# Macaron block (FFN, butterfly mixer, FFN) on 8 cores: how the blocks of T are prepared beside the units, where the second chunk joins, and what the second FFN's first slabs wait for

## The chip, the cores and the metric

One Trainium2 chip, all 8 cores. Each core runs the same program on its own 2048 of the 16384 tokens, with no exchange between cores. The metric is the device time of the slowest core in microseconds (us), lower is better.

## The reference, cut to what matters

`x` is 16384 tokens (4 x 4096) of 2048 channels, float32. `fwht` is the normalised Walsh-Hadamard transform over the last axis.

```python
def ffn(x):                       # _L0_ffn_ref
    x = fwht(x * SU_ug) / SCALE                       # this is T, 2048 wide
    x_up   = x @ W_up.T   * (Wscale_ug[:INTER] * SCALE)    # 8192 wide
    x_gate = x @ W_gate.T * (Wscale_ug[INTER:] * SCALE)
    x = silu(x_gate) * x_up
    x = fwht(x * SU_dp) / SCALE
    return x @ W_down.T * (Wscale_dp * SCALE)

def mixer(u):                     # _L0_attn_ref
    state = apply_butterfly(u @ W_b_rank @ W_b_state, A_factors)   # rank 64, 256 states
    return state @ W_c_rank @ W_c_model + D_vec * u

x = x + 0.5 * ffn(layernorm(x))
x = x + mixer(layernorm(x))
x = x + 0.5 * ffn(layernorm(x))
```

The same FFN weights serve both FFNs.

## The kernel before, in words

**Layout.** Channels lie on partitions, tokens on the free axis. A core's 2048 tokens are 8 blocks of 256 (`PB`), 4 sets `s` of 512 (`SC`), and 2 chunks `c` of 1024. `place(j)` is the j-th 8 KB (per partition) of the big buffer BIG; T of chunk 0 lies in places 0 to 6, T of chunk 1 in places 7 to 13. Behind them come three slabs of weights (`SL`, `NSLAB`), the slabs' sums (`SUMS`) and scratch.

**A program with a plan.** All instructions are put out by one Python program that appends to five lists, one for each engine (`Prog.st`, `Prog.dma`). A wait is on the count that another instruction leaves in a semaphore. The order of each engine's list is fixed there. Work in the background is a set of generators (`put`); `tick(us)` moves a planned clock on and resumes each generator whose time has come, and `yield 3.0` in one of them means: go on not before 3 us later. A bare `yield` means the next tick. The main stream calls `tick(8 * MM)` = 1.73 us after each 8 matmuls, so times are rounded up to ticks of 1.73. The planned clock sets only the order of the lists; on the chip each engine runs its list as its semaphores allow.

**Preparing T.** Each block goes through `norm` (two casts on ScalarE, 16 matmuls with ones, two subtractions on VectorE, two squares, 16 matmuls, square root, reciprocal) and `transform` (8 groups of two matmuls with the Hadamard matrix and an eviction, then butterflies for distances 8, 4, 2 and 1, an add and a subtract each over 2048 columns, L376 and L379), and is stored to `tsc` with a DMA of the SP queue. `prep_first` does it for the first FFN: it asks for x (`x_halves`, two DMAs on SP), yields 45 us times `S.pace`, then norm and transform. `prep_mixed` does norm, the mixer, the store of x2, norm and transform. A set of buffers (`Set`) serves one block at a time: S0 (PXF, PXC, PXA) takes the even blocks, S1 (inside the places of chunk 1) the odd ones in the first FFN, S2 in the second, until set 3, whose two blocks (6 and 7) both go through S0 beside the second FFN's units. `S.pace` is 0.4 for blocks 2 and 3 and goes back to 1.0 in `t7_rest` when they are done.

**Up product (`u_phase`).** 64 tiles of 128 + 128 rows of W_up and W_gate. A slab (`load`, L84 through POOL's queue, 2 MB of float32 cast to 1 MB of bf16) holds one tile. A unit is one tile with one chunk as a Strassen product (`strassen`, L694): 7 products of 8 matmuls of 128x512, with 6 combination adds on VectorE (L703), one copy and two silu on ScalarE and two multiplications (L862) on VectorE. It needs 5 sums of the slab (`sums`, L779, VectorE), made once per slab, and 5 sums of T over two halves each (`t7_sums`, L662). In the first FFN tiles 0 to 11 (`ALONE`) run first with set 0 alone as plain products (L797). Then tiles up to `FIRST[f]` run with chunk 0 alone, then chunk 1 **joins**: from tile `FIRST[f]` on each slab serves both chunks; after tile 63 the early tiles are loaded again for chunk 1 alone, and the early 12 for set 1 and chunk 1. So `FIRST` = 32 gives 64 + 20 + 24 = 108 slabs, 36 in the second FFN 64 + 36 = 100.

**The join.** When chunk 1 is first needed, `need` waits in the plan until its four blocks are stored, puts `t7_build` (four loads of T, a pause of 20 us, ten sums) and ticks until it is done. `need1` is the same for the second FFN.

**Beside it.** `side0` runs blocks 2, 4 and 6 in S0, waits for T of chunk 1, and then runs `fold`: W_down is transformed in 64 units of 8 matmuls (L507), casts (L511), a load and a store each (`wdn` to `fsc`, then `fsc` to `dsc`). The down product of the first FFN (`d_phase`, L971) reads `dsc` through a ring of four places (`ring_emit`, SP queue) and holds the preparation of sets 0 to 2 of the second FFN. At its end `ahead` puts `head()`, the `start` of the second FFN's `u_phase`, which loads slabs 0, 1 and 2 at planned distances of 14 us. The second FFN's down product is `Down7` (L1194).

## Time and profile before

| what | us |
|---|---|
| three runs | 5574.59, 5505.05, 5411.33 (median 5505.05) |
| the profiled execution, its own time | 5411.29 |
| its span on the slowest core (5) | 5409.7 |
| spans of the other cores | 5380.2 to 5404.4 |

| stage on core 5 | from | to |
|---|---|---|
| blocks 0 and 1, then tiles 0 to 11 with set 0 | 0 | 171 |
| chunk 0 alone, blocks 4 to 7 beside it | 171 | 524 |
| both chunks, fold beside them | 524 | 1425 |
| chunk 1 alone, the fold's end beside it | 1425 | 1580 |
| rest of the up product | 1580 | 1920 |
| down product, preparation of the second FFN | 1920 | 2926 |
| second FFN: chunk 0 alone, blocks 6 and 7 | 2926 | 3433 |
| both chunks | 3450 | 4108 |
| chunk 1 alone | 4108 | 4545 |
| second down product | 4545 | 5410 |

How to read the rows. PE is TensorE (matmuls), PEld its weight loads, DVE VectorE, ACT ScalarE, POOL GpSimd, SP the sync engine; a name with q is that engine's queue of DMA issues. L694 is a line of the kernel; most DMAs are issued by one helper at L84. `out<-in` are buffers. "PEclk" is the granted TensorE clock as a share of full speed, "DMA" the mean busy share of the core's 16 DMA engines. In a timeline a row is start, length, engine, line, operation, and in brackets the idle time before it and what ended it. In the waits a row says who waited for whom: total us, times, longest. Ends of matmuls are modelled and overlap, so times per matmul are taken from counts over a stretch or from starts. A few records of matmuls may be missing.

### The profile page before, as it was taken

What the parts mean: (1) busy time and instruction counts of PE and PEld (TensorE: products, weight loads), DVE (VectorE), ACT (ScalarE), POOL (GpSimd) and SP (SyncE); (2) the same over time, 40 slices, a digit from 0 to 9 for tenths busy, and PEclk for the clock granted to TensorE, in tenths of its full rate; (3) what the DMA queues carried; (4) which work ended last, traced back from release to release, by engine and by line L of the source; (5) the groups of instructions that cost most, each with busy time, mean ns of one, the idle gap of its engine ahead of it and who ended that gap; (6) DMA issues with size and microseconds to landing.
All of it is one profiled execution on the core that took longest, in us unless ns stands there. A gap on an engine that the chain in (4) does not pass through costs nothing.

```text
span 5409.7 us, 69392 instructions; the slowest of 8 cores (5380.2 to 5409.7 us)
## 1 busy us (share of the span) xinstructions
PE 5124.2 (95%) x23972; PEld 2350.6 (43%) x23972; DVE 3118.1 (58%) x4405; ACT 1011.2 (19%) x1460; POOL 128.6 (2%) x247
## 2 busy tenths in 40 slices
PE   6788999999999999999998999999999999997998
PEld 3343444444444444444453444444444444443443
DVE  5777455555563611243345787655557776766766
ACT  3221343444331100111110222111111111000000
POOL 0000000000000000000000000000000000000000
PEclk8999999999999999999999999999999999998999
DMA  7566888877987766686856556332335555776765
GB/s 164 102 131 134 169 190 177 193 199 187 210 185 143 160 206 216 225 277 212 289 193 163 105 119 152 76 68 61 69 63 129 109 111 157 233 221 213 244 221 187
DMA packets 378590, 901.16 MB, mean 167 GB/s; under 512 B 30150, under 2 KB 259526, under 8 KB 311494
## 3 DMA queue, kind: packets, MB, share of 16 engines
q1 hardware_dynamic: 224760, 512.43, 30.2%
q0 software_dynamic: 34992, 252.00, 27.5%
q10 hardware_dynamic: 118496, 132.29, 7.0%
q8 instruction: 200, 3.28, 0.3%
q14 instruction: 142, 1.16, 0.1%
HBM read 918.95 MB, written 229.64 MB: 212 GB/s over the span
## 4 chain that ended last, share of the span: by engine, by line
PE 76%; DMA 10%; DVE 8%; issue 4%; ACT 1%; SPq 1%; ACTq 0%; DVEq 0%; POOLq 0%; POOL 0%
PE P L694 44%; PE P L971 15%; PE P L1194 11%; PE P L797 2%; DMA BIG<-dsc 2%; PE P L281 2%; DMA PXF<-fsc 2%; PE P L507 2%; DVE BIG L703 1%; DMA fsc<-PXC 1%; SPq L84 1%; DMA fsc<-PXA 1%; DVE BIG L779 1%; DVE BIG L1209 1%; DMA PXF<-wdn 1%
## 5 line engine op out<-in xcount | busy, mean ns | idle before, releaser
L694 PE MATMUL P<-BIG 128*128 128x512 bf16 x13664 | 3074.2, 381 | 78.6 <-DVE BIG L703 50.9
L694 PEld LDWEIGHTS P<-BIG 128*128 128x128 bf16 x13664 | 1338.0, 98 | 1703.6 <-issue 138.0
L971 PE MATMUL P<-BIG 128*128 128x512 bf16 x4096 | 903.6, 380 | 33.0 <-DMA BIG<-dsc 33.0
L703 DVE TENSOR_TENSOR BIG<-P,BIG 128x512 f32<-128x512 f32 x976 | 670.2, 687 | 287.1 <-PE P L694 124.0
L703 DVE TENSOR_TENSOR BIG<-BIG,P 128x512 f32<-128x512 f32 x488 | 333.7, 685 | 537.9 <-ACT BIG L872 452.0
L779 DVE TENSOR_TENSOR BIG<-BIG 128x1024 bf16<-128x1024 bf16 x920 | 615.1, 684 | 36.5 <-DMA BIG<-wug 18.2
L971 PEld LDWEIGHTS P<-BIG 128*128 128x128 bf16 x4096 | 399.8, 98 | 511.9 <-issue 51.2
L1194 PE MATMUL P<-BIG 128*128 128x512 bf16 x1792 | 399.3, 384 | 28.6 <-DVE BIG L1209 22.0
L872 ACT ACTIVATE BIG<-P,WSCG 128x512 bf16<-128x512 f32 x244 | 168.1, 689 | 902.0 <-PE P L694 901.9
L862 DVE SCALAR_TENSOR_TENSOR GST<-P,WSCU,BIG 128x512 bf16<-128x512 f32 x244 | 183.1, 750 | 250.2 <-ACT BIG L877 238.9
L1194 PEld LDWEIGHTS P<-BIG 128*128 128x128 bf16 x1792 | 175.9, 99 | 249.1 <-issue 45.7
L707 ACT COPY BIG<-P 128x512 f32<-128x512 f32 x244 | 144.2, 591 | 718.0 <-DVE BIG L779 331.0
L1194 PE MATMUL P<-BIG,PXF 128*128 128x512 bf16 x1024 | 236.2, 385 | 25.5 <-DVE BIG L1209 23.6
L937 DVE SCALAR_TENSOR_TENSOR BIG<-P,WSC,BIG 128x512 f32<-128x512 f32 x64 | 45.1, 746 | 365.0 <-PE P L971 365.0
L877 ACT ACTIVATE BIG<-BIG,WSCG 128x512 bf16<-128x512 f32 x244 | 176.1, 722 | 275.8 <-DVE BIG L703 275.8
L862 DVE SCALAR_TENSOR_TENSOR GST<-BIG,WSCU 128x512 bf16<-128x512 f32 x244 | 183.4, 752 | 42.9 <-DVE BIG L703 42.9
L84 POOL DMA_DIRECT2D BIG<-wug x208 | 109.8, 528 | 4063.6 <-PE P L694 2041.3
L511 ACT CAST PXC<-P 128x512 bf16<-128x512 f32 x256 | 146.3, 586 | 276.8 <-PE P L507 184.4
L511 ACT CAST PXA<-P 128x512 bf16<-128x512 f32 x256 | 146.5, 586 | 275.3 <-PE P L507 188.1
L1209 DVE TENSOR_TENSOR BIG<-P,BIG 128x512 f32<-128x512 f32 x184 | 125.7, 686 | 124.3 <-PE P L1194 121.6
L797 PE MATMUL P<-BIG 128*128 128x512 bf16 x768 | 169.3, 381 | 21.3 <-DVE BIG L368 20.2
L1223 ACT COPY BIG<-P 128x512 f32<-128x512 f32 x46 | 26.9, 586 | 829.6 <-PE P L1194 570.6
(101 smaller groups left out, 2385.2 us busy)
## 6 DMA issues: line engine op xcount, KB each, us to landing
BIG<-wug POOLq DMA_DIRECT2D x208, 1024.0 KB, 10.0
BIG<-dsc SPq DMA_DIRECT2D x133, 1024.0 KB, 7.0
gsc<-GST ACTq DMA_DIRECT2D x512, 128.0 KB, 7.3
PXF<-wdn POOLq DMA_DIRECT2D x32, 1024.0 KB, 11.7
PXF<-fsc SPq DMA_DIRECT2D x32, 1024.0 KB, 9.1
BIG<-gsc SPq DMA_DIRECT2D x32, 1024.0 KB, 6.7
BIG<-gsc SPq DMA_DIRECT2D x128, 256.0 KB, 6.8
outT<-BIG ACTq DMA_DIRECT2D x92, 256.0 KB, 4.7
```

The lines of the kernel that those rows point to most:

```text
L84: (lambda e, o=out, i=in_: e.dma_start(out=o, in_=i), ws, (sem, 16)))
L511: t_ev = p.st("scalar", lambda e, b=b, i=i, j=j: e.copy(fou[j][:, i * 512:(i + 1) * 512], PS[b][:, :]), [t, out_tok[j]])
L694: tok[j] = p.st("tensor", lambda e, k=k, l=a(j, k), r=b(j, k): e.matmul(PS[bank][:, :], l, r, start=(k == 0 and not acc), stop=(k == n - 1 ...
L703: return p.st("vector", lambda e: e.tensor_tensor(o, x, y, op), waits)
L779: tk[j] = p.st("vector", lambda e, o=o, x=x, y=y, op=op: e.tensor_tensor(o, x, y, op), [sl_tok[i], sum_free[i % 2], tk.get(2) if j == 6 el ...
L797: "tensor", lambda e, b=b, c0=c0, k=k: e.matmul(PS[b][:, :], L[:, c0:c0 + 128], t7_cols(T[k // 8], k % 8), start=(k == 0), stop=(k == NKT ...
L862: tg = p.st("vector", lambda e, t=t: e.scalar_tensor_tensor(g, src, WSCU[:, t:t + 1], sl, OP.mult, OP.mult), x + [t_vec, gst_tok[slot]])
L872: cb["s1"] = p.st("scalar", lambda e, t=t: e.activation(si[0], PS[where][:, :], AF.Silu, scale=WSCG[:, t:t + 1]), [tok, tmp["s1"], t_wscg])
L877: ts = p.st("scalar", lambda e, t=t: e.activation(si[1], where, AF.Silu, scale=WSCG[:, t:t + 1]), [tok, tmp["s2"], t_wscg])
L971: t9=t9: e.matmul(PS[b][:, :], W[:, c0:c0 + 128], gr, start=t0, stop=t9),
L1194: tok[j] = p.st("tensor", lambda e, l=l, r=r, m=m: e.matmul(PS[bank][:, :], l, r, start=(m == a and not acc), stop=(m == b - 1), skip_grou ...
L1209: return p.st("vector", lambda e: e.tensor_tensor(o, x, y, op), waits)
```

## The change

- A block's set asks for x of its next block (`next(first[blk + 2])`, in the second FFN `next(after)`) right behind its norm; the yield of 45 us (30 us) that follows the request is used up there.
- `Set` gets a `step`: each step of `transform` yields `S.step` us, in place of the next tick. `paced` runs blocks 2 and 3 as before, then blocks 4 to 7 with pace 1.2 and step 4.0. Set 3 of the second FFN runs with pace 1.3 and step 4.0.
- `t7_build` of chunk 1 is no longer put at the join: it follows the last block in `side0` (ahead of `fold`) and in `last()`. Its four loads go out 6 us apart and its ten sums 3 us apart.
- `FIRST` goes from (32, 36) to (36, 48): 112 slabs in each FFN.
- In the second FFN slabs 1 and 2 wait for the load of the ring that was issued last.

```diff
--- before.py
+++ after.py
@@ -21,7 +21,7 @@
 NRING = 4
 NITEM = 10
 NSLAB = 3
-FIRST = (32, 36)
+FIRST = (36, 48)
 ALONE = (12, 0)
 MM = 0.216
 C8192 = 1.0 / float(np.sqrt(8192.0))
@@ -290,7 +290,7 @@
                 self.X, self.XC, self.A, self.RS, self.i = x, xc, xa, rs, i
                 self.b0, self.b1 = banks
                 self.x_free, self.xc_free, self.a_free, self.rs_free = [], [], [], []
-                self.pace = 1.0
+                self.pace, self.step = 1.0, 0.0
 
         def kh(ap):
             return ap.rearrange("p (k t) -> p k t", k=8)
@@ -352,7 +352,7 @@
                     bc(S.RS, 2), OP.mult), [t, t_v, t_rs])
                 ps_free[b] = [t_ev]
                 t_pe = t
-                yield
+                yield S.step
             S.rs_free = [t_ev]
             src, dst = A, XC
             tl = [t_ev, t_pe]
@@ -375,12 +375,12 @@
                 dv = dst.rearrange("p (n h w) -> p n h w", h=2, w=dc * PB)
                 t1 = p.st("vector", lambda e, sv=sv, dv=dv: e.tensor_tensor(
                     dv[:, :, 0, :], sv[:, :, 0, :], sv[:, :, 1, :], OP.add), tl)
-                yield
+                yield S.step
                 t2 = p.st("vector", lambda e, sv=sv, dv=dv: e.tensor_tensor(
                     dv[:, :, 1, :], sv[:, :, 0, :], sv[:, :, 1, :], OP.subtract))
                 tl = [t2]
                 src, dst = dst, src
-                yield
+                yield S.step
             S.xc_free = [t2]
             t = p.dma("sync", sPT[S.i], tsc[f][blk], A, [t2])
             S.a_free = [t]
@@ -398,9 +398,11 @@
             yield 45.0 * S.pace
             t_xc, t_v, t_rs = yield from norm(S, t_x, False)
             S.x_free = [t_xc]
+            if 4 <= blk + 2 < NBLK:
+                next(first[blk + 2])
             yield from transform(S, 0, blk, t_xc, t_v, t_rs)
 
-        def prep_mixed(S, blk):
+        def prep_mixed(S, blk, after=None):
             s = blk // 2
             X, XC, A = S.X, S.XC, S.A
             t_x = x_halves(S, x1s, blk, [S.x_free, x1_tok[s]])
@@ -452,6 +454,8 @@
             yield 3.0
             t_xc, t_v, t_rs = yield from norm(S, [t_x2, t_x2], False)
             S.x_free = [t_xc, t_st]
+            if after is not None:
+                next(after)
             yield from transform(S, 1, blk, t_xc, t_v, t_rs)
 
         spad_free = [None, None]
@@ -671,8 +675,9 @@
             tk = {}
             for j in (1, 4, 5, 6):
                 tk[j] = t7_load(f, c, j, [free.get(j)])
-            yield 20.0
-            yield from t7_sums(c, tk, free, (0, 2, 3, 5, 6))
+                yield 6.0
+            for _ in t7_sums(c, tk, free, (0, 2, 3, 5, 6)):
+                yield 3.0
             toks[c] = tk
 
         def t7_cols(slot, k):
@@ -823,7 +828,8 @@
 
             def start(waits=()):
                 for i in range(3):
-                    load(i, waits)
+
+                    load(i, waits if al or i == 0 else ring_tok[-1:])
                     yield 0.0 if al else 14.0
                 yield from sums(0)
 
@@ -1281,7 +1287,6 @@
         def t7_rest():
             while len(t_tok[0][1]) < 2:
                 yield
-            S0.pace = S1.pace = 1.0
             tk = {j: list(t_tok[0][j in (4, 5)]) for j in (1, 4, 5, 6)}
             st5 = p.dma("sync", sPT[0],
                         tsc[0][2:4, :, 0:2048].rearrange("b p x -> p b x"),
@@ -1293,10 +1298,7 @@
                 yield
             yield from t7_sums(0, tk, {6: alone_over[0]}, (6,))
 
-        def need(f, c, free):
-            wait_t(f, c)
-            if c == 1:
-                put(t7_build(f, c, toks, free()))
+        def need(c):
             while toks[c] is None:
                 tick(2.0)
 
@@ -1321,7 +1323,7 @@
                 if pos < 8:
                     gpos[0][pos] = g_load(0, 0, pos, pos)
 
-        up = u_phase(0, toks, lambda c: need(0, c, set1_over), ring_a, ring_b)
+        up = u_phase(0, toks, need, ring_a, ring_b)
         head = next(up)
         put(first[0])
         put(first[1])
@@ -1331,14 +1333,22 @@
         t_wbrb = p.dma("gpsimd", sC[1], WBRB[:, :], wbr)
 
 
+        def paced(S, gens):
+
+            yield from gens[0]
+            S.pace, S.step = 1.2, 4.0
+            yield from in_turn(gens[1:])
+            S.pace, S.step = 1.0, 0.0
+
         def side0():
-            yield from in_turn([first[2], first[4], first[6]])
-            while toks[1] is None:
+            yield from paced(S0, [first[2], first[4], first[6]])
+            while len(t_tok[0][2]) < 2 or len(t_tok[0][3]) < 2:
                 yield
+            yield from t7_build(0, 1, toks, set1_over())
             yield from fold()
 
         put(side0())
-        put(in_turn([first[3], first[5], first[7]]))
+        put(paced(S1, [first[3], first[5], first[7]]))
         put(t7_rest())
         for _ in up:
             pass
@@ -1356,7 +1366,13 @@
                 put(late(prep_mixed(S0, 2 * s)))
                 put(late(prep_mixed(S2, 2 * s + 1)))
             else:
-                put(late(in_turn([prep_mixed(S0, 2 * s), prep_mixed(S0, 2 * s + 1)])))
+                def last():
+                    yield 10.0
+                    S0.pace, S0.step = 1.3, 4.0
+                    final = prep_mixed(S0, 2 * s + 1)
+                    yield from in_turn([prep_mixed(S0, 2 * s, final), final])
+                    yield from t7_build(1, 1, toks1, item2[0])
+                put(last())
 
         def before(s):
             if s == 0:
@@ -1370,8 +1386,6 @@
         item2 = []
 
         def need1(c):
-            wait_t(1, c)
-            put(t7_build(1, c, toks1, item2[0]))
             while toks1[c] is None:
                 tick(2.0)
```

## Rows read from the trace of the kernel before

**Rows 1.** The page: PE's busy time, and its granted clock in 40 slices

```profile
PE 5124.2 (95%) x23972; PEld 2350.6 (43%) x23972; DVE 3118.1 (58%) x4405; ACT 1011.2 (19%) x1460; POOL 128.6 (2%) x247
...
PEclk8999999999999999999999999999999999998999
```

**Rows 2.** Windows by stage: from:to, length, busy us (x instructions), PEclk, DMA share, GB/s

```profile
171.00:524.00 353.00, 292.78 (x1371) 134.90 (x1368) 263.95 (x357) 78.27 (x88) 11.61 (x22) 0.94 0.61 122
...
1425.00:1580.00 155.00, 149.44 (x683) 67.05 (x682) 93.38 (x143) 60.22 (x107) 5.80 (x11) 0.99 0.98 223
...
2926.00:3433.00 507.00, 480.99 (x2296) 223.84 (x2296) 400.57 (x584) 116.90 (x142) 19.01 (x36) 0.99 0.58 124
3433.00:3450.00 17.00, 15.75 (x60) 6.41 (x61) 16.10 (x19) 1.66 (x3) 0.00 (x0) 0.81 0.01 4
3450.00:4108.00 658.00, 658.00 (x3050) 298.31 (x3049) 385.08 (x575) 108.60 (x164) 14.77 (x28) 1.00 0.34 73
```

**Rows 3.** Windows of line L694 alone, PE

```profile
171.00:524.00 353.00, 270.24 (x1176) 0.94 0.61 122
2926.00:3433.00 507.00, 461.18 (x2072) 0.99 0.58 124
```

**Rows 4.** Timeline of PE near 213 us: start, length, engine, line

```profile
212.25 1.91 PE L281 MATMUL P<-PXA,ONES 128*128 128x256 bf16 x16
213.99 1.91 PE L281 MATMUL P<-BIG,ONES 128*128 128x256 bf16 x16
```

**Rows 5.** Waits of PE, 171 to 545 us: total, times, longest

```profile
PE P L694 <- DVE BIG L703: 34.5, 14, 5.8
PE P L281 <- ACT PXA L308: 13.3, 1, 13.3
PE P L694 <- DVE BIG L662: 5.5, 1, 5.5
```

**Rows 6.** Timeline of PE, waits in brackets: up to the first join

```profile
184.76 3.57 PE L281 MATMUL P<-PXA,ONES 128*128 128x256 bf16 x16 [13.31 <-ACT PXA L308]
...
404.31 7.41 PE L694 MATMUL P<-BIG 128*128 128x512 bf16 x24 [5.44 <-DVE BIG L703]
...
524.54 10.62 PE L694 MATMUL P<-BIG 128*128 128x512 bf16 x40 [5.52 <-DVE BIG L662]
```

**Rows 7.** Windows of 20 us, one of a burst on VectorE

```profile
400.00:420.00 20.00, 12.36 (x40) 4.73 (x41) 18.73 (x23) 1.41 (x2) 0.53 (x1) 0.74 0.36 65
```

**Rows 8.** Timeline of SP: when x is asked for

```profile
109.31 0.85 SPq L84 DMA_DIRECT2D PXF<-ub  x2
...
273.24 3.40 SPq L84 DMA_DIRECT2D PXF<-ub  x2
```

**Rows 9.** Timeline of DVE at the first join

```profile
522.04 11.82 DVE L662 TENSOR_TENSOR BIG<-BIG 128x2048 bf16<-128x2048 bf16 x10
```

**Rows 10.** Windows of 100 us, one of single units with nothing beside them

```profile
4300.00:4400.00 100.00, 100.00 (x465) 45.34 (x464) 70.60 (x108) 16.68 (x25) 4.76 (x9) 1.00 0.56 107
```

**Rows 11.** Tile wug, 180 to 430 us

```profile
DMA to landing us min/median/max: 8.3/9.9/22.0
```

**Rows 12.** Timeline of PE: two waits of the fold's matmuls

```profile
588.82 0.59 PE L507 MATMUL P<-PXF,H128B 128*128 128x512 bf16 x1 [8.45 <-ACT PXC L511]
...
1431.60 0.38 PE L507 MATMUL P<-PXF,HKB 128*128 128x512 bf16 x1 [2.98 <-DMA PXF<-fsc]
```

**Rows 13.** Timeline at the end of the first down product, and its DMA issues

```profile
2871.02 1.59 POOL L84 DMA_DIRECT2D BIG<-wug  x3 [999.66 <-DVE BIG L379]
...
2889.40 7.07 PE L971 MATMUL P<-BIG 128*128 128x512 bf16 x32 [1.59 <-DMA BIG<-dsc]
2907.43 15.47 PE L971 MATMUL P<-BIG 128*128 128x512 bf16 x64 [10.96 <-DMA BIG<-dsc]
...
BIG<-dsc SPq DMA_DIRECT2D x4, 1024.0 KB, 23.5
BIG<-wug POOLq DMA_DIRECT2D x3, 1024.0 KB, 24.3
```

## The prediction, made before the change was run

> **What bounds the kernel now.** I read the page first, then the windows by stage, then the waits and the timeline of the stages that fall short. The page gives PE 95% busy, and a clock granted in full except in a few slices [rows 1]; the reader is to see that nothing is to be gained where PE runs through. The windows by stage give the measure of running through: 3050 matmuls of 128x512 in 658 us, 0.2157 us each, at clock 1.00 and no idle time [rows 2]. A Strassen unit has 56 of them, so 12.08 us. A matmul of 128x256 takes 1.74 us for 16, 0.109 us each (the distance of the two starts) [rows 4]. With these two prices each stage has a floor.
>
> The stage ahead of the first join (171 to 524 us) holds 1371 matmul records, 1176 of them L694, which is 21 units [rows 2, 3]; the other 195 are norms and transforms of x. Floor: 1176 x 0.2157 + 195 x 0.109 = 253.7 + 21.3 = 275. It takes 353, so 78 us are lost. The same stage of the second FFN (2926 to 3433) holds 2072 of L694, 37 units, and 224 others [rows 2, 3]: 446.9 + 24.4 = 471.3 of 507, 35.7 lost. The 17 us behind it hold 60 matmuls, 12.9 us worth: 4.1 lost [rows 2]. These two stages are all that the larger parts of the change touch.
>
> What is lost in the first: PE waits 34.5 us in 14 pieces for VectorE's combination adds, 13.3 us once for a cast on ScalarE, and 5.5 us for the sums of T at the join [rows 5]. The timeline shows where: at 184.8 (the cast), at 404 amid a burst, at 524.5 (the join) [rows 6]. In the burst VectorE is 18.73 of 20 us busy, and the granted clock is 0.74 [rows 7]: the engine idled just before, so the loss has a second part, matmuls at the lower of the two levels. Bursts come from the generator of `transform`: it gives one butterfly half at every tick of the plan (1.73 us), for both sets at once.
>
> **Part by part.** *Prefetch of x and pacing (first FFN).* The row of SP shows that x of blocks 4 and 5 was asked for at 109.3, as soon as the norm before had freed X, though its instruction stands behind the whole transform; x of blocks 6 and 7 was asked for at 273.2, behind the store of T [rows 8]. So for blocks 4 and 5 nothing moves in time on SP; for 6 and 7 the two loads of each set leave ahead of the store that they stood behind. What changes is the plan: each of blocks 4 to 7 loses its 45 us of planned waiting, and its steps are spread: norm 9 yields of 3.6 to 4.8 us (5.18 us each when rounded up to ticks), transform 16 of 4.0 (also 5.18), so 130 us a block instead of some 106. Blocks 2 and 3 end at planned 59 us, blocks 4 to 7 then take 260 (to 319), the T build 4 x 6.9 + 10 x 3.46 = 62 (to 381). The join is planned at 12 x 6.91 + 25 x 12.1 = 385. So T of chunk 1 is there in time, with nothing to spare.
>
> VectorE pays for it: it was busy 264 us in the stage [rows 2]. To that come 11.8 us for the ten sums of T, now inside the stage [rows 9], and four more units with their slab sums at 8.5 us each (70.6 us for 465/56 = 8.3 units [rows 10]), 34 us: 310. PE's floor with 25 units is 275 + 48.3 = 323. VectorE at 0.96 of PE's floor is the tight point of the change. Where it is fullest now it reaches 0.94 [rows 7], and 310/0.94 = 330, so at least 7 us are lost. From above: if its share of the stage stayed at 264/353 = 0.748, the stage would take 310/0.748 = 414, with 91 lost. The nearest row is the second FFN's stage, with one stream of preparation beside single units and a share of 0.79: it loses 7.3% of its floor on top, 35.7 of 471 [rows 2]; 7.3% of 323 is 24. I add 9 for what stays of the cast's wait at 185 (its x is ready sooner, but VectorE still waits for a store of T there) and take 33, between 12 and 91. Before, the same 25 units ended at 353 + 3.5 (the matmuls after the wait at the join, 40 in 10.62 us [rows 6], and a small wait) + 48.3 = 404.8 from the stage's start; now 323 + 33 = 356. **Gain 48.5 us**, 70 at best, a loss of 9 at worst.
>
> What is late next at the join: the plan is tight, so one or two sums of T may be put out with no unit between them, 2 us; it is in the 9. The four loads of T now go out 6 us apart, in place of four at once, so the slab that they share the DMA engines with is less delayed.
>
> The Trainium skill speaks against this part: "SBUF — State Buffer" (the box on the trap where DVE blocks DMA) says that a DMA issued from GpSimd's queue waits for its descriptors while VectorE runs an instruction in a two-port mode. The slabs are issued there, and VectorE gets fuller. The trace does not bear it out as a cost: in this stage, with VectorE at 0.75 and up to 0.94, a slab landed in 9.9 us at the median and 22.0 at most [rows 11]. By the rule a slab would be late; with three in flight it has some 36 us, so the sum is the same by the one and by the other unless landings double.
>
> *FIRST (first FFN), 32 to 36.* Four more slabs (208 to 212), their loads and 20 sums, hidden where nothing else runs: the row of single units has PE 100 of 100 us busy with VectorE at 0.71 [rows 10]. But the fold keeps its length (512 ticks, some 73 units) while the joint stage has 8 units fewer, so 8 more units of chunk 1 alone run beside the fold. That pairing has a row: 1425 to 1580, DMA share 0.98, 683 matmuls, floor 147.3 of 155, so 7.7 us lost over 11.4 units [rows 2], 0.68 a unit. **Cost 5.5 us.** From below it is nothing; from above it is a wait like that of the fold's matmul at 588.8, 8.45 us, behind a store of the fold, where later ones waited 2.98 [rows 12].
>
> *Second FFN: step, x of the last block, T build, 36 to 48.* One stream. Planned: 10 + 245 + 210 for two blocks, 62 for T, 527 in all, against a join at 49 x 12.1 = 593: 66 us to spare, so the join's wait goes for certain (5.5 us of wait and its slow matmuls are within the 35.7 + 4.1). VectorE: 400.6 + 12 x 8.5 + 11.8 = 514 of a floor of 471.3 + 145 = 616, 0.83. Bounds: at best 8 us lost, at worst its share stays at 0.79 and 651 are needed, 35 lost. The bursts are gone and the density hardly rises: I take 20 lost. Before 40 were: **gain 20 us**, from 5 to 32. The 12 more slabs and their 41 us of sums lie in stages where PE never waited.
>
> *Slabs 1 and 2 behind the ring.* At 2871.0 all three slabs are issued while the down product still needs two loads of its ring; these take 23.5 us at the median, and PE waits 1.59 and 10.96 us for them, the last until 2907.4 [rows 13]. With two of three megabytes of weights moved behind the last ring load, that one should land about ten microseconds sooner. Both waits go, and some 2 us of matmuls at the lower clock. POOL's queue now waits for the last ring load with slabs 1 and 2; behind them stands only slab 3, which needs slab 0's unit to end. Slab 1 is needed one unit after slab 0, 12 us later, and is asked for before the stage begins. **Gain 14 us**, from 0 (if the loads of T beside it are what delays the ring) to 15.
>
> **Sum.** 48.5 - 5.5 + 20 + 14 = 77 us. The profiled execution took 5411.3 us (span 5409.7), so 5334 us. The three runs shown lie from 5411 to 5575 with a median of 5505, 94 us above the profiled one; the forecast is for an execution like the profiled one, and at the place of that median the same gain reads 5428.
>
> **Rivals.** *A, VectorE does not get fuller.* Its steps stand in one program with PE's, and each sum put between two combination adds delays the release of a bank; then the share of each stage stays. First stage 414 against 404.8 (loss 9), second 651 against 656 (gain 5), ring 14, fold -5.5: gain 4, 5407 us. For it: PE's 34.5 us of waits are all of this kind, and two sets still step at the same tick. Against: they come in bursts, with stretches of 20 us at full rate between.
>
> *B, the smooth plan works as in the best stretches.* First stage loses 12 (gain 70), second 8 (gain 32), ring 14, fold -3: 113 us, 5298. For it: with full use the clock stays up; against: VectorE at 0.96 of PE's floor.
>
> *C, slower: the fold beside single slabs.* DMA share is 0.98 there already. If the backlog grows over 19 units instead of 11, each of the some 6 or 7 fold units in the 8 added ones waits like the one at 588.8, 8.45 us and the clock's fall behind it (0.26 of 20 us, 5.2): 7 x 13.7 = 96 against a gain of 82: 5425 us. It decides from 12 us a fold unit. Against: waits there were 3 us and less.
>
> *D, the prefetch does nothing:* on SP it does nothing for blocks 4 and 5, as said; this is in the forecast.
>
> **Chances.** The forecast 0.57 (its own range 5300 to 5370), A 0.20, B 0.17, C 0.06. The range goes from 5280 (within B) to 5435, which takes in A, C and the place of the median. Faster by over 2% (about what a measurement of this kernel can tell from no change) means under 5303: all of B and a small part of the forecast, 0.22. Slower by over 2% would need C with twice its price: 0.04. Within 2%: 0.74.
>
> **What would show it.** Right: no wait of PE for L662 at either join; 25 units in some 356 us from 171 us on with VectorE near 0.87; no wait of L971 for dsc near 2890 to 2907; the windows beside the fold's end at 0.98 DMA share and over 430 matmuls in 100 us. Wrong: new waits of PE for L703 spread evenly over the first stage (A), waits for fsc in every fold unit behind the joint stage (C), or a wait for slab 1 or 2 at the start of the second FFN.

## The result, and the profile after

| | before | after |
|---|---|---|
| median | 5505.05 us | 5467.2 us (5 runs) |
| lowest | 5411.33 us | 5383.99 us |
| ratio, 95% interval | 1 | 0.9935 [0.9910, 0.9960] |
| profiled execution, own time | 5411.29 us | 5383.99 us |
| its spans, mean of 8 cores | 5393.95 us | 5363.2 us |

So the change is a gain of some 35 us by the ratio (0.0065 x 5411), and 27 us between the two profiled executions, where 77 was forecast. Some executions, both medians among them, are disturbed (the cores of a die at a lower granted clock) and are left out of comparisons; the only profiles of the experiments `e1_ring` (on cores 0 to 3) and `e7_step0` fell in such executions and are read only as far as said there.

The page of after, PE's busy time and clock, beside [rows 1]; the page numbers lines some 5 higher now (L699 is the Strassen matmul, L708 its combination add, L784 a slab's sum, L712 its copy, L868 the multiplication, L977 the down product, L802 and L818 the plain product of tiles 0 to 11 and its multiplication, L511 and L515 the fold's matmul and cast; L666 is the sum of T).

```profile
PE 5122.2 (95%) x23972; PEld 2350.1 (44%) x23972; DVE 3163.0 (59%) x4485; ACT 1011.7 (19%) x1460; POOL 137.6 (3%) x263
...
PEclk8999999999999999999999999999999999998999
```

PE's work is the same 23972 matmuls. VectorE has the 80 instructions of 16 more slabs. The stage ahead of the first join, now with 36 - 12 = 24 units and the first of the join, and the window beside the fold, answering to [rows 2]; below them L699 alone in the first, as [rows 3].

```profile
171.00:562.00 391.00, 342.22 (x1610) 156.20 (x1609) 305.95 (x418) 79.51 (x96) 14.84 (x28) 0.97 0.60 126
...
1300.00:1400.00 100.00, 98.05 (x452) 43.98 (x451) 57.43 (x87) 40.76 (x73) 3.18 (x6) 1.00 0.95 219
1400.00:1500.00 100.00, 95.69 (x442) 42.87 (x441) 59.65 (x91) 39.21 (x70) 3.71 (x7) 1.00 0.98 224
```

```profile
171.00:562.00 391.00, 319.73 (x1414) 136.99 (x1415) 0.97 0.60 126
```

VectorE's busy time, 306 us, is what was forecast (310). The length isn't: 391 us for 1414 / 56 = 25.25 units, with VectorE at 306 / 391 = 0.78. Of the 196 other matmuls 36 are 128x512 ones of L802 and L511 and 160 are 128x256, so the floor is 1450 x 0.2157 + 160 x 0.109 = 330, and 61 us are lost. What PE waited for in it, as [rows 5], and where, as [rows 6]:

```profile
PE P L699 <- DVE BIG L708: 28.4, 23, 4.9
PE P L699 <- DVE BIG L784: 14.0, 1, 14.0
PE P L699 <- ACT BIG L712: 6.2, 7, 1.5
```

```profile
177.62 0.81 PE L802 MATMUL P<-BIG 128*128 128x512 bf16 x3
192.46 3.15 PE L699 MATMUL P<-BIG 128*128 128x512 bf16 x7 [14.03 <-DVE BIG L784]
```

The wait for the cast at 184.8 is gone, and at the same place stands one of 14.0 us for a slab's sum. The waits for combination adds are shorter and more: 28.4 us in 23 pieces after 34.5 in 14. No wait for a sum of T at the join is left. VectorE's timeline shows what the slab's sum stood behind:

```profile
172.91 2.56 DVE L666 TENSOR_TENSOR BIG<-BIG 128x2048 bf16<-128x2048 bf16 x2 [7.14 <-DMA tsc<-BIG]
175.38 2.28 DVE L317 TENSOR_TENSOR PXC<-PXF,P 128x2048 bf16<-128x2048 f32 x1
177.58 2.28 DVE L317 TENSOR_TENSOR BIG<-BIG,P 128x2048 bf16<-128x2048 f32 x1
179.78 0.75 DVE L818 SCALAR_TENSOR_TENSOR GST<-P,WSCU,BIG 128x512 bf16<-128x512 f32 x1
185.44 0.75 DVE L818 SCALAR_TENSOR_TENSOR GST<-P,WSCU,BIG 128x512 bf16<-128x512 f32 x1 [4.91 <-ACT BIG L812]
186.10 2.28 DVE L317 TENSOR_TENSOR PXC<-PXF,P 128x2048 bf16<-128x2048 f32 x1
188.30 2.28 DVE L317 TENSOR_TENSOR BIG<-BIG,P 128x2048 bf16<-128x2048 f32 x1
190.49 1.22 DVE L666 TENSOR_TENSOR BIG<-BIG 128x2048 bf16<-128x2048 bf16 x1
191.63 0.69 DVE L784 TENSOR_TENSOR BIG<-BIG 128x1024 bf16<-128x1024 bf16 x1
```

Four L317 (the norm's subtractions of blocks 4 and 5, 2.28 us each) now stand in VectorE's list ahead of the first sums of the first Strassen slab, and the whole list waited 7.14 us behind a sum of T for a store.

Where T of chunk 1 is built, first SP, then VectorE:

```profile
475.44 2.88 SPq L84 DMA_DIRECT2D BIG<-tsc  x4
...
DMA to landing us min/median/max: 17.0/34.6/42.9
```

```profile
506.20 1.22 DVE L666 TENSOR_TENSOR BIG<-BIG 128x2048 bf16<-128x2048 bf16 x1 [6.52 <-DMA BIG<-tsc]
...
516.38 1.23 DVE L666 TENSOR_TENSOR BIG<-BIG 128x2048 bf16<-128x2048 bf16 x1 [2.90 <-DMA BIG<-tsc]
```

The four loads go out together (they all wait for the last store of T, whatever the plan puts between them), land 17.0 to 42.9 us later, and the sums, planned 3 us apart, wait for them at the head of VectorE's list: combination adds stand behind.

The end of the down product, as [rows 13], with its issues of loads:

```profile
2859.53 0.53 POOL L84 DMA_DIRECT2D BIG<-wug  x1 [1009.43 <-DVE BIG L379]
2892.58 1.06 POOL L84 DMA_DIRECT2D BIG<-wug  x2 [32.52 <-DMA BIG<-dsc]
```

```profile
2889.45 15.91 PE L977 MATMUL P<-BIG 128*128 128x512 bf16 x64 [6.22 <-DMA BIG<-dsc]
2908.83 8.79 PE L699 MATMUL P<-BIG 128*128 128x512 bf16 x40 [3.46 <-DVE BIG L784]
```

```profile
BIG<-dsc SPq DMA_DIRECT2D x4, 1024.0 KB, 18.5
```

POOL holds slabs 1 and 2 back 32.5 us as meant; the ring's load lands sooner (18.5 after 23.5 us at the median), but not in time: PE still waits 6.2 us for it.

**A clock by stages.** To compare eleven kernels I take, on each core, the issue of the slab that a unit's end releases (POOL's timeline), and the mean over the 8 cores. A: tiles 0 to 11 done. J: the first tile done with both chunks, which is tile 36 where the join is at 36; where it is at 32 (39), four (three) units of 12.08 us are added (taken off), so that the work up to J is the same 26 units. U: the last slab of the first up product. R: the first unit of the second FFN. K: as J for the second join, at 48. E: the last slab of the second FFN.

| kernel | A | J | U | R | K | E |
|---|---|---|---|---|---|---|
| before | 170.5 | 586.6 | 1856.7 | 2928.5 | 3582.1 | 4493.7 |
| after | 177.9 | 568.4 | 1847.4 | 2912.1 | 3551.9 | 4463.3 |
| e2_ffn1 | 177.6 | 572.9 | 1854.8 | 2926.0 | 3579.4 | 4490.9 |
| e3_ffn2 | 170.6 | 587.9 | 1862.1 | 2936.8 | 3575.2 | 4487.2 |
| e4_norm_late | 170.1 | 574.1 | 1855.7 | 2917.1 | 3555.4 | 4466.9 |
| e6_t_later | 177.5 | 565.9 | 1845.3 | 2911.3 | 3553.6 | 4465.1 |
| e8_first32 | 177.8 | 580.2 | 1871.3 | 2939.5 | 3577.9 | 4489.6 |
| e9_step0_held | 177.8 | 588.5 | 1876.8 | 2939.5 | 3577.5 | 4488.9 |
| e10_no_butterfly | 177.0 | 542.7 | 1828.5 | 2895.0 | 3539.6 | 4451.0 |
| e11_hold | 177.3 | 551.3 | 1833.5 | 2898.4 | 3536.2 | 4447.6 |
| e12_hold_gap | 177.5 | 548.5 | 1834.2 | 2901.0 | 3546.0 | 4457.3 |

Each row is one execution, and two pairs show how far such rows can be trusted. `e2_ffn1` has after's instructions up to U, and its J is 4.5 us later (3.3 of them from the first Strassen unit) and its U 7.4 us later; `e3_ffn2` has before's, and its J is 1.3 and its U 5.4 us later. Differences below some 5 us at J and 7 us at U therefore show nothing by themselves.

The difference of after and before, stage by stage, against the terms of the forecast's sum:

| stretch | gain, us | forecast |
|---|---|---|
| start to J | 18.2 | 48.5 |
| J to U | -8.9 | -5.5 |
| U to R | 7.1 | 14 |
| R to K | 13.8 | 20 |
| K to E | 0.2 | 0 |
| sum | 30.4 | 77 |

The sum agrees with the 30.8 us by which the mean span fell. Every term has its sign and gives less than forecast; two thirds of what is missing is in the first. The 3.4 us between -8.9 and -5.5 are within the scatter just given.

### The profile page after: what moved, and what is told of

Read it like the earlier page. It is cut to its first block, busy times and chain, and to the rows that moved or that the text cites. A ratio compares the mean times of both kernels' runs of the same rounds, so it can differ in the third digit from the quotient of the medians.

```text
span 5382.3 us, 69545 instructions; the slowest of 8 cores (5332.6 to 5382.3 us)
## 1 busy us (share of the span) xinstructions
PE 5122.2 (95%) x23972; PEld 2350.1 (44%) x23972; DVE 3163.0 (59%) x4485; ACT 1011.7 (19%) x1460; POOL 137.6 (3%) x263
## 3 DMA queue, kind: packets, MB, share of 16 engines
q1 hardware_dynamic: 224760, 512.43, 30.4%
## 4 chain that ended last, share of the span: by engine, by line
PE 78%; DMA 8%; DVE 7%; issue 4%; ACT 1%; SPq 1%; ACTq 1%; DVEq 0%
PE P L699 45%; PE P L977 15%; PE P L1200 11%; PE P L802 2%; DMA BIG<-dsc 2%; PE P L281 2%; PE P L511 2%; DVE BIG L708 1%; DMA fsc<-PXA 1%; DMA PXF<-fsc 1%; SPq L84 1%; DMA BIG<-tsc 1%; DVE BIG L784 1%; DVE BIG L1215 1%; DMA tsc<-BIG 1%
## 5 line engine op out<-in xcount | busy, mean ns | idle before, releaser
L699 PE MATMUL P<-BIG 128*128 128x512 bf16 x13664 | 3065.2, 380 | 72.5 <-DVE BIG L708 43.1
L699 PEld LDWEIGHTS P<-BIG 128*128 128x128 bf16 x13664 | 1334.8, 98 | 1690.0 <-issue 122.0
L977 PE MATMUL P<-BIG 128*128 128x512 bf16 x4096 | 906.5, 381 | 33.8 <-DMA BIG<-dsc 33.8
L708 DVE TENSOR_TENSOR BIG<-P,BIG 128x512 f32<-128x512 f32 x976 | 670.7, 687 | 248.2 <-ACT BIG L712 125.1
L784 DVE TENSOR_TENSOR BIG<-BIG 128x1024 bf16<-128x1024 bf16 x1000 | 669.7, 685 | 26.9 <-DMA BIG<-wug 8.3
L708 DVE TENSOR_TENSOR BIG<-BIG,P 128x512 f32<-128x512 f32 x488 | 333.4, 687 | 502.9 <-ACT BIG L878 434.4
L977 PEld LDWEIGHTS P<-BIG 128*128 128x128 bf16 x4096 | 400.6, 98 | 514.8 <-issue 55.6
L1200 PE MATMUL P<-BIG 128*128 128x512 bf16 x1792 | 400.2, 384 | 27.8 <-DVE BIG L1215 21.3
L868 DVE SCALAR_TENSOR_TENSOR GST<-P,WSCU,BIG 128x512 bf16<-128x512 f32 x244 | 183.2, 751 | 248.6 <-ACT BIG L883 238.0
L712 ACT COPY BIG<-P 128x512 f32<-128x512 f32 x244 | 144.5, 592 | 731.8 <-DVE BIG L784 361.4
L868 DVE SCALAR_TENSOR_TENSOR GST<-BIG,WSCU 128x512 bf16<-128x512 f32 x244 | 183.4, 752 | 43.0 <-DVE BIG L708 43.0
L515 ACT CAST PXA<-P 128x512 bf16<-128x512 f32 x256 | 146.8, 587 | 280.7 <-PE P L511 181.2
L515 ACT CAST PXC<-P 128x512 bf16<-128x512 f32 x256 | 146.6, 587 | 271.9 <-PE P L511 176.5
L802 PE MATMUL P<-BIG 128*128 128x512 bf16 x768 | 171.3, 384 | 23.0 <-DVE BIG L368 20.2
## 6 DMA issues: line engine op xcount, KB each, us to landing
PXF<-fsc SPq DMA_DIRECT2D x32, 1024.0 KB, 11.8
```

What stands on the lines that cost most here:

```text
L515: t_ev = p.st("scalar", lambda e, b=b, i=i, j=j: e.copy(fou[j][:, i * 512:(i + 1) * 512], PS[b][:, :]), [t, out_tok[j]])
L699: tok[j] = p.st("tensor", lambda e, k=k, l=a(j, k), r=b(j, k): e.matmul(PS[bank][:, :], l, r, start=(k == 0 and not acc), stop=(k == n - 1 ...
L708: return p.st("vector", lambda e: e.tensor_tensor(o, x, y, op), waits)
L784: tk[j] = p.st("vector", lambda e, o=o, x=x, y=y, op=op: e.tensor_tensor(o, x, y, op), [sl_tok[i], sum_free[i % 2], tk.get(2) if j == 6 el ...
L802: "tensor", lambda e, b=b, c0=c0, k=k: e.matmul(PS[b][:, :], L[:, c0:c0 + 128], t7_cols(T[k // 8], k % 8), start=(k == 0), stop=(k == NKT ...
L868: tg = p.st("vector", lambda e, t=t: e.scalar_tensor_tensor(g, src, WSCU[:, t:t + 1], sl, OP.mult, OP.mult), x + [t_vec, gst_tok[slot]])
```

## The experiments

### The parts one by one

`e1_ring`: before, with the gate on slabs 1 and 2 alone.

```diff
             def start(waits=()):
                 for i in range(3):
-                    load(i, waits)
+                    load(i, waits if al or i == 0 else ring_tok[-1:])
```

> The kernel before with one edit: slabs 1 and 2 of the second FFN wait for the last ring load. My theory now: the gate takes away about half of the two waits for dsc near 2890 and 2907 (6 of 12.5 us), because the loads of T beside it delay the last ring load too: the whole gets shorter by 7 us (5404). Rival, the prediction's: 14 us. Rival on the other side: the gate gives nothing (the 7 us that the changed kernel gained between the two FFNs come from a luckier ring elsewhere).

Its lowest run took 5423.37 us, before's lowest on the same chip 5413.4, so the whole time shows no gain. Cores 4 to 7 of its profile took from U to R 2922.4 - 1861.2 = 1061.2 us, before's same cores 1071.0. On the same cores PE's waits for dsc fell from 13.8 to 2.8 us on the mean. So the gate alone is worth some 7 to 10 us; in the other kernels U to R takes 1061 to 1068 where the gate is in (after 1064.7), and 1071.2 (`e2_ffn1`) and 1074.7 (`e3_ffn2`) where it isn't.

`e2_ffn1`: after, with the second FFN as before (`FIRST` 36, 36; no gate, no `last()`, T of its chunk 1 built at the join). `e3_ffn2`: before, with the second FFN's part (`FIRST` 32, 48; the steps and `last()` for set 3), no gate.

```diff
# e2_ffn1, against after
-FIRST = (36, 48)
+FIRST = (36, 36)
...
-                    load(i, waits if al or i == 0 else ring_tok[-1:])
+                    load(i, waits)
...
-                put(last())
+                put(late(in_turn([prep_mixed(S0, 2 * s), prep_mixed(S0, 2 * s + 1)])))
# e3_ffn2, against before
-FIRST = (32, 36)
+FIRST = (32, 48)
...
-                put(late(in_turn([prep_mixed(S0, 2 * s), prep_mixed(S0, 2 * s + 1)])))
+                put(last())
```

> The changed kernel's first FFN (prefetch, paced, T of chunk 1 ahead of the join, joining tile 36) with the second FFN and the ring as before. My theory now: the first FFN gained only 9 us as a mean of the cores (last slab issue 1856.7 to 1847.4), so the whole is 10 us shorter: 5401, ratio 0.998. PE's waits in the stage ahead of the join: one of 12 to 14 us for the first slab sums, two or three of 2 to 5 us where VectorE waits for a load of T, and 20 small ones. Rival, the prediction's: 43 us shorter, 5368.

> The changed kernel's second FFN alone (steps of 4 us, x of the last block asked for early, T of chunk 1 ahead of the join, joining tile 48), first FFN and ring as before. My theory now: 14 us shorter as in the stage times of the changed kernel, 5397, ratio 0.9974. Rival, the prediction's: 20 us, 5391. Rival: the 12 more slabs cost elsewhere and the whole gains less than 8.

Ratios to before: 0.9981 [0.9962, 1.0001] and 0.9969 [0.9933, 1.0006]. Multiplied, with some 8 us for the gate (0.9985), they give 0.9935, after's ratio. Taken together their intervals reach 0.4% to either side, so this shows only that no part spoils another by much over 20 us. In stages: the first FFN's part brings J 13.7 us forward (after: 18.2) and loses 11.8 of it again by U. The second FFN's part takes R to K from 653.6 to 638.4 us, 15.2.

### The first stage: what holds it

`e4_norm_late`: after, with blocks 4 and 5 held back 18 us in the plan.

```diff
             yield from gens[0]
+            yield 18.0
             S.pace, S.step = 1.2, 4.0
```

> The changed kernel with 18 planned us put back between blocks 2, 3 and 4, 5. Theory: in the changed kernel the norm of blocks 4 and 5 stands in VectorE's queue between the wait for the store of T and the first slab sums, so PE waits 14 us for L784 at 178 us; put back, the norm falls behind the first sums and that wait goes down to 3 us, but the old one of 13 us for the cast comes back: no difference over 5 us to the changed kernel (5384). Rival: the wait is the norm's alone, and the kernel gets 10 us faster (5374).

Lowest 5405.2 us, no ratio. A is back at 170.1; the wait for the slab's sum is gone and the one for the cast is back, 13.0 us (after the change 14.0, before 13.3); J is 5.7 us later than in after (from A to J 404.0 us in place of 390.5, after an A 7.8 us sooner). So the hole near 185 us isn't a matter of when x arrives: one of the two stands there by the order of the lists.

`e5_sum5_late`: after, with the sum of T that waits for the store put behind.

```diff
-            yield from t7_sums(0, tk, {5: st5}, (0, 2, 3, 5))
+            yield from t7_sums(0, tk, {5: st5}, (0, 2, 3))
+            yield 10.0
+            yield from t7_sums(0, tk, {5: st5}, (5,))
             toks[0] = tk
```

> The changed kernel with one edit: the two sums of T that wait for the store of T (place 5) come 10 planned us later, behind two more adds and norms in VectorE's queue. Theory: they block VectorE for 7 us at 166 to 173 and so delay the norm and the first slab sums; moved back, PE's wait of 14 us for L784 at 178 us falls to under 8, and the join's tile ends 6 us sooner (562 as a mean of the cores against 568.4). Rival: VectorE's work itself (norm of two blocks, 9 us of subtractions, ahead of the slab sums) makes the wait, which stays over 11 us.

0.9932 [0.9908, 0.9956], after's own value. VectorE's wait for the store fell from 7.1 to 1.7 us, PE's for the slab's sum from 12.7 to 7.3 (mean of cores 0 to 3), while its waits for combination adds and copies rose from 31.8 to 35.0. On these cores J is 566.7, after's 567.6 (cores 4 to 7 have a lower granted clock, 0.972 to 0.980, and are not compared). 5.4 us of the visible wait were taken away, 3.2 came back as other waits, and J moved by 1 us, which is within the scatter.

`e10_no_butterfly` prices VectorE's work. It leaves out the butterflies of blocks 4 to 7 of the first FFN (32 instructions, some 36 us), so their T isn't transformed fully; all `yield`s stay.

```diff
+            skip = f == 0 and s >= 2
             for dc in (8, 4, 2, 1):
+                if skip:
+                    yield S.step
+                    yield S.step
+                    continue
```

> The changed kernel without the butterflies of blocks 4 to 7 in the first FFN (their T is left untransformed): 32 instructions of 1.22 us, 36 us of VectorE's work gone from the stage ahead of the first join, the yields kept. Asks for the price of VectorE's work there. Theory: of the 55 us that PE loses in this stage some 35 are for VectorE, and they grow with its work: the join comes 15 to 20 us sooner (550), half a us for each us of VectorE. Rival: VectorE has idle time enough, the waits are of single chains, and the join moves less than 6 us.

0.9920 [0.9876, 0.9964]; J 25.7 us sooner than in after. PE's waits, and the window up to its join:

```profile
PE P L706 <- DVE BIG L791: 17.6, 1, 17.6
PE P L706 <- DVE BIG L715: 8.1, 6, 2.2
PE P L706 <- ACT BIG L719: 4.3, 5, 1.8
```

```profile
171.00:540.00 369.00, 337.06 (x1623) 157.98 (x1622) 274.36 (x391) 81.37 (x100) 14.28 (x27) 0.98 0.67 134
```

36 us less work on VectorE, at a share of 0.78, gives 25.7: 0.7 us per us at most. VectorE bounds this stage, though it is busy only 0.78 of it. The waits for combination adds (L715 here) went from 25.9 to 8.8 us on the mean core (8.1 on the core shown); the one before the first Strassen unit stays, 14.6 on the mean (12.1 in after), 17.6 on the core shown. Not all of the 25.7 us is the work itself. Without butterflies T is stored and loaded earlier (the four loads leave at 410.80), and VectorE's waits for them, 6.7 us on the mean core in after, are gone. When tile 31 is done the kernel is 18.1 us ahead, and the last 7.6 us come in the units where after waits for T. So the price of VectorE's work lies between 0.5 and 0.7 us per us.

`e9_step0_held` takes the spreading back (step 0 in both FFNs), with the fold held until the join is planned, so that mainly the bursts differ (T of chunk 1 is also there sooner, and VectorE waits 0.1 us for it where after waits 6.7). `e7_step0` is the same without that hold.

```diff
-            S.pace, S.step = 1.2, 4.0
+            S.pace, S.step = 1.2, 0.0
...
-                    S0.pace, S0.step = 1.3, 4.0
+                    S0.pace, S0.step = 1.3, 0.0
...
             yield from t7_build(0, 1, toks, set1_over())
+            while unit["n"] < 12 + 25:
+                yield
             yield from fold()
```

> The changed kernel with steps of 0 in place of 4 us in both FFNs (bursts, as before), all else kept: asks what the spreading gives. Theory: VectorE's added work costs PE nearly the same spread or in bursts, since with 0.78 of the stage busy only part can hide behind waits of VectorE that it has anyway; the bursts cost 10 us more in the first stage (join 578) and 4 in the second. The prediction's view: the bursts cost 20 to 25 more in the first stage (join 590).

> The changed kernel with steps of 0 us in both FFNs, as in the run before it with bursts, but with the fold held until 25 units of chunk 0 are done. In that run the fold started at some 490 us, beside single units, and PE waited 31 us in three pieces for the fold's casts. Theory: most of the 76 us that it lost against the changed kernel came from the fold beside single slabs, and the bursts alone cost 10 to 15: join at 580 (568.4 in the changed kernel), the whole 5400, ratio 0.996. Rival: the bursts are the cost, join at 620 and later, ratio over 1.005.

`e7_step0` came out at 1.0108 [1.0011, 1.0205], some 1% slower than before; with the hold 0.9993 [0.9973, 1.0013]. In `e9_step0_held` J is 588.5, 20.1 us later than in after and 15.6 later than in `e2_ffn1`: that is what the spreading is worth in the first FFN, more than I expected of it. It is also before's J (586.6): the early x, T built ahead of the join and the later join bring nothing at J without the spreading. In the second FFN, where this kernel has step 0 too, R to K takes 638.0 us, after's 639.8: there the spreading shows no gain. The rest of `e7_step0`'s loss comes from the fold: blocks 6 and 7 end sooner, T of chunk 1 too, and `side0` goes straight on to the fold, beside chunk 0's last single units. In its profile I read only what the waits are for:

```profile
514.59 0.59 PE L511 MATMUL P<-PXF,H128B 128*128 128x512 bf16 x1 [10.81 <-ACT PXC L515]
...
559.81 0.59 PE L511 MATMUL P<-PXF,H128B 128*128 128x512 bf16 x1 [11.65 <-ACT PXC L515]
```

Such waits, before the join, stand in neither before nor after. This is rival C's mechanism, at a place where the change as made doesn't put the fold.

`e8_first32`: after, with the first join at 32 as before.

```diff
-FIRST = (36, 48)
+FIRST = (32, 48)
```

> The changed kernel with the first join back at tile 32, so T of chunk 1 is not there when it is asked for. In the plan the join then waits for blocks 6 and 7 and T, 48 us with no unit. Theory: VectorE, not PE, holds up this stage, so the waiting of PE at the join gives back half of what it costs: VectorE's work has the stage to itself, PE's waits before it fall away at the end; the join (taken to 36 tiles) ends 20 us later than the changed kernel's, at 588, and the whole is 15 us longer (5399). Rival: the full 48 us are lost (5430).

0.9968 [0.9951, 0.9985]; J at 580.2, 11.8 us later than in after. The join comes before T:

```profile
515.70 3.57 PE L699 MATMUL P<-BIG 128*128 128x512 bf16 x8 [12.60 <-DVE BIG L666]
521.44 4.93 PE L699 MATMUL P<-BIG 128*128 128x512 bf16 x16 [2.17 <-DVE BIG L666]
```

So the later join pays for the slower preparation: the spread T without it has PE standing still, 12.6 us in one piece on this core and 15.7 us for sums of T on the mean core. From J to U this kernel takes 1291.1 us, the longest of all, with before's `FIRST`.

### Better orders

`e6_t_later`: after, with a pause of 30 us between the four loads of T and the first sum, in both FFNs, and the first join at 39.

```diff
-FIRST = (36, 48)
+FIRST = (39, 48)
...
                 yield 6.0
+            yield 30.0
             for _ in t7_sums(c, tk, free, (0, 2, 3, 5, 6)):
```

> The changed kernel with 30 planned us between the four loads of T of chunk 1 and its sums, and the join at tile 39. Theory: in the changed kernel the four loads go out at once and land in some 30 us, and VectorE stands 9 us for them with the combination adds behind it, PE 8 to 10 us; here no wait of VectorE for a load of T is left, and the join (taken back to 36 tiles by 12.08 us a unit) ends 8 us sooner: 560. Against it 2 us more beside the fold; the whole 5378. Rival: the waits of PE for the combination adds come from the spread steps alone, and the join ends no sooner than 566.

0.9909 [0.9881, 0.9937]. VectorE waits for no load of T any more; J is 2.5 us sooner than in after, which alone is within the scatter. But when tile 31 is done the kernel is still 2.5 us behind after (its wait before the first Strassen unit is 15.4 us on the mean core, after's 12.1), and the 5.0 us between come in the units where after waits for T. PE's waits for combination adds fall from 25.9 to 22.4 us on the mean core.

`e11_hold`: after, with the subtractions of blocks 4 and 5 (but not the casts and matmuls ahead of them) held 14 us in the plan. All that follows them in blocks 4 to 7, and the building of T, moves back by these 14 us with them.

```diff
-                self.pace, self.step = 1.0, 0.0
+                self.pace, self.step, self.hold = 1.0, 0.0, 0.0
...
-            yield 3.0 * S.pace
+            yield 3.0 * S.pace + S.hold
+            S.hold = 0.0
...
             yield from gens[0]
-            S.pace, S.step = 1.2, 4.0
+            S.pace, S.step, S.hold = 1.2, 4.0, 14.0
```

> The changed kernel with 14 planned us between the first 16 matmuls of ones of blocks 4 and 5 and the subtractions that use them; the casts and the matmuls stay early. Theory: PE's wait of 14 us at 178 has two halves: the norm of x in VectorE's queue ahead of the sums of T and of slab 12, and ScalarE's squares. With the subtractions behind the first sums both this wait and the old one for the cast are away: a wait of 5 us or less, the join 8 us sooner (560), the whole 5376. Rival: the norm's later matmuls wait in its place, and the join is no sooner than 566.

0.9944 [0.9900, 0.9989] and a lowest time of 5371.37 us, against 5410.11 of before on the same chip. The first stage's waits and window:

```profile
PE P L700 <- DVE BIG L709: 18.1, 19, 3.3
PE P L700 <- ACT BIG L713: 14.4, 7, 10.2
PE P L700 <- DVE BIG L785: 4.3, 2, 2.9
```

```profile
171.00:545.00 374.00, 337.00 (x1597) 154.78 (x1596) 303.01 (x414) 79.39 (x96) 14.24 (x27) 0.98 0.62 128
```

J is 17.1 us sooner than in after, twice what I expected, with the same work on VectorE (303 us, share 0.81). On the mean core PE's waits for a slab's sum fell from 12.1 to 3.5 us and those for combination adds from 25.9 to 18.6, while those for ScalarE's copies rose from 6.8 to 9.8 (one of 10.2 on this core); VectorE's waits for the loads of T fell from 6.7 to 1.5. In VectorE's list the first two sums of the slab now stand ahead of the first two subtractions, and all sums that the first unit needs ahead of the other two:

```profile
179.71 0.69 DVE L785 TENSOR_TENSOR BIG<-BIG 128x1024 bf16<-128x1024 bf16 x1
180.31 1.22 DVE L667 TENSOR_TENSOR BIG<-BIG 128x2048 bf16<-128x2048 bf16 x1
181.44 0.69 DVE L785 TENSOR_TENSOR BIG<-BIG 128x1024 bf16<-128x1024 bf16 x1
182.04 2.28 DVE L318 TENSOR_TENSOR PXC<-PXF,P 128x2048 bf16<-128x2048 f32 x1
184.24 2.28 DVE L318 TENSOR_TENSOR BIG<-BIG,P 128x2048 bf16<-128x2048 f32 x1
186.44 4.08 DVE L785 TENSOR_TENSOR BIG<-BIG 128x1024 bf16<-128x1024 bf16 x6
...
191.83 2.28 DVE L318 TENSOR_TENSOR PXC<-PXF,P 128x2048 bf16<-128x2048 f32 x1
```

How much of the 17.1 us is this order? At the end of the second Strassen unit the kernel is 7.6 us ahead of after, and 10 to 11 us ahead of `e2_ffn1` and `e6_t_later`, which start the stage as after does. The rest comes later, 5 us of it by tile 21 and the last 5 in pieces up to J, where the blocks' steps meet other units than before. Which of the shifts in the plan brings that, no run here separates.

`e12_hold_gap` is both together.

```diff
-FIRST = (36, 48)
+FIRST = (39, 48)
...
+            yield 30.0
             for _ in t7_sums(c, tk, free, (0, 2, 3, 5, 6)):
...
-            S.pace, S.step = 1.2, 4.0
+            S.pace, S.step, S.hold = 1.2, 4.0, 14.0
```

> The same with the gap of 30 us between the loads of T of chunk 1 and its sums, and the join at tile 39. Theory: the gains add, 8 us from the one and 2 to 3 from the other: join (taken to 36 tiles) at 558, the whole 5373, ratio 0.990. Rival: no gain over the changed kernel beyond noise (0.9935).

0.9919 [0.9885, 0.9952], lowest 5375.09 us. J is another 2.8 us sooner (within the scatter), but R to K takes 645.0 us, in `e11_hold` 637.8. Whether the pause in the second FFN costs this is open: `e10_no_butterfly`, without a pause, has 644.6, with the second FFN of after (639.8). By the clock of stages `e11_hold` is the best of these (E at 4447.6, 15.7 us before after's), by the ratios `e6_t_later`; the intervals overlap, and the runs don't order the three. The pause in the first FFN alone, with the hold, wasn't tried.

## Why the prediction was wrong, point by point

**The step that failed** is the size of one term of the sum: "it loses 7.3% of its floor on top, ... 7.3% of 323 is 24. I add 9 for what stays of the cast's wait ... and take 33, between 12 and 91". By the clock of stages, before lost 80.7 us in this stage (A to J with its own 22 units took 367.8 us, floor 22 x 12.08 + 21.3 = 287.1) and after lost 58.6 (390.5 us, floor of 26 units 331.9, since 32 of the norm's matmuls, 3.5 us, now stand ahead of A), and 3.9 more ahead of A: 62.5 where I took 33. VectorE's busy time was right, 306 for 310. Wrong was what share it can reach. I took the loss of a stage with one stream and a share of 0.79 and applied it to one that would have needed 0.87; the stage stayed at 0.78. That is no fixed ceiling, for with another order of the same work it reached 0.81 (`e11_hold`). `e10_no_butterfly` gives the price that was missing: 0.5 to 0.7 us for each us of VectorE's work. The term's two parts:

- The combination adds: 25.9 us of waits on the mean core (28.4 on core 2), in pieces of under 5 us on most cores (the longest is 6.7, on core 5), for adds whose place in VectorE's list is among the butterflies, the slabs' sums and the sums of T. Rival A named this ("each sum put between two combination adds delays the release of a bank") and its sign, new small waits spread over the stage, is there. A's time isn't: it had the first stage lose 9 us, and it gained 18. The truth lies between the forecast (356 us for 25 units) and A (414): by the clock of stages they took 378.4 us from A on, 386 with the 7.4 us by which A is later. B, which had this stage lose 12 us, is further off still. The bursts were a real cost, as the forecast said: `e9_step0_held` shows 20 us for them.
- The hole at 185 us: I gave it 9 us "for what stays". It stayed whole, 12.1 us on the mean core where the cast's was 12.7, with 3.9 us lost ahead of A on top; it was passed from ScalarE's cast to VectorE's sums. "VectorE still waits for a store of T there" was right (7.14 us) but, by `e5_sum5_late`, not what decides; the order of the norm's subtractions and the first slab's sums does (`e11_hold`: the wait fell to 3.5 us, and 7.6 us were gained by the end of the second unit).

**The join**: no wait of PE for a sum of T: right. "The four loads of T now go out 6 us apart": wrong, all four left within 2.88 us from 475.44 on, since the plan's distances are nothing to a queue whose head waits for the last store. "With nothing to spare" was right, and its price, which I had in the 9 us, was VectorE waiting 6.52 and 2.90 us with the adds behind it.

**The fold, 5.5 us**: 8.9 measured, and as much or more in all of the other kernels with the new first FFN (J to U 1279.4 to 1291.1 us, before's 1270.1). The term was for moving the join from 32 to 36, and that is not what the runs show: `e8_first32`, with the join at 32, takes longest. The windows beside the single units are as forecast (DMA 0.95 and 0.98; 452 and 442 matmuls in 100 us). The extra was elsewhere: from 600 to 1000 us PE waits, on the mean of 8 cores, 15.2 us in after and 6.7 in before, most of it for the fold's casts (L515). On core 2 the waits of PE and of ScalarE there:

```profile
PE P L511 <- ACT PXA L515: 9.8, 4, 4.5
PE P L511 <- ACT PXC L515: 2.7, 4, 1.1
```

```profile
ACT PXC L515 <- DMA fsc<-PXC: 19.4, 6, 4.3
```

The casts wait in turn for stores of the fold. That is rival C's kind of wait, in the joint stage and far below C's price. Why it grew there, the runs don't say.

**The ring, 14 us**: 7.1 measured, some 10 with the gate alone (`e1_ring`). "Both dsc waits go" was wrong. On cores 4 to 7 of before they sum to 16.3, 12.6, 10.9 and 15.5 us, in after 5.6, 3.0, 6.1 and 2.5 remain (6.2 on core 2). The mechanism was right. What stays may be the loads of T and of x1 that share the DMA engines with the last ring load, as the lower end of my range had it; taking those away wasn't tried.

**The second FFN, 20 us**: 13.8, 15 to 16 in six of the kernels that share this part, and 9 to 11 in the other three. The join's wait went, as said. What stays is waits for adds and copies, 10.5 us in 10 and 4.0 in 4 on the slowest core: nearly as before (12.7 in 12, 5.1 in 4). So "the bursts are gone" bought nothing here, as `e9_step0_held` shows, and what was gained is the join.

**The prefetch**: it "does nothing" for blocks 4 and 5, and the x of blocks 6 and 7 was asked for at 188.46 in place of 273.24 [rows 8], with no wait for either. Rival D holds: what acts in this change is the spreading, with the order in the lists.

**The slabs' landings** stood at 8.7 / 9.2 / 19.1 us (least, median, most) in the first stage of after, with VectorE at 0.78; [rows 11] had 9.9 and 22.0. The prediction set this against the Trainium skill ("SBUF — State Buffer", the trap where DVE blocks DMA). What the box names is an instruction of VectorE in a two-port mode, not a fuller VectorE, and no row here shows the mode of an instruction; so the landings show that a share of 0.78 costs the slabs nothing, as forecast, and don't test the rule.

**Range and median.** The forecast for the place of before's median was 5428; the measured median is 5467.2. The profiled execution took 5383.99, 50 us over the forecast for it: 30 of the 50 are the first stage's term, 7 the ring, 6 the second stage, 3 the fold, and 3 that the slowest core gained less than the mean. The range was built round the profiled execution and stretched to a median of three runs that lay 94 us above it; a range for a median has to be moved by all of that distance.

## What to carry to other kernels

A stage is bounded by an engine long before that engine is full, if the engine's list also holds the work that releases the other's buffers: here each us of VectorE's background work cost 0.5 to 0.7 us at a share of 0.78. So estimate such a stage by taking work out, not by the share it could reach, and count what stands ahead of the first consumer at a seam between two stages, since a wait removed there is passed on to the next one in the list unless the order is changed. A planned distance between DMAs spreads nothing when they wait for the same event: see whether their issues lie apart in the trace.

## What the runs showed that I had not expected

Holding four subtractions of 2.28 us back behind the first sums of a slab, and all that follows them by the same 14 planned us, brought the join 17 us forward (`e11_hold`), though the wait that it was made for went down by only 8.6 us. Four loads of T of 1 MB each, issued in 2.9 us, took 17.0 to 42.9 us to land, where a slab took 9.2 at the median. And a stage that ends sooner doesn't hand all of it on: PE's waits between 600 and 1000 us, for the fold's casts, were 6.7 us in before, 15.2 in after and 22.2 in `e10_no_butterfly`, whose J is the earliest, though `e6_t_later` (10.7, with an early J) and `e9_step0_held` (19.5, with before's J) show that the start doesn't set them.
